# Three engines' orders rewritten in the second edge pipeline of a four-layer graph network

## What is computed

```python
x = layernorm(x + L0(x, edges, edge_attr_128))   # softmax-weighted messages, MLP
x = layernorm(x + L1(x, edges))                  # sum over edges, MLP, batch norm
x = layernorm(x + L2(x, edges, edge_attr_20))    # filtered messages, dense o1, shifted softplus, dense o2
x = layernorm(x + L3(x, edges))                  # two mean-aggregating convolutions
```

## Time and profile before

| | us |
|---|---|
| median of 3 runs (lowest to highest) | 2390.36 (2384.64 to 2391.72) |
| the profiled execution, its own time | 2387.5 |
| its span in the trace | 2385.8 |
| busy, TensorE / VectorE / ScalarE / GpSimd | 2083.7 / 1989.8 / 1791.3 / 1516.3 |

### The profile page before, as it was taken

The page is one execution under the profiler, slowest core; times in us unless marked ns, Lnnn a source line. Parts: engine busy times, 40 slices in busy tenths (PEclk is TensorE's granted clock), DMA queues, the critical chain, the costliest instruction groups (busy, mean ns, idle before and its releaser), DMA issues. The chain is left out here.

```text
span 2385.8 us, 45628 instructions
## 1 busy us (share of the span) xinstructions
PE 2083.7 (87%) x14016; PEld 1738.5 (73%) x14016; DVE 1989.8 (83%) x2942; ACT 1791.3 (75%) x3691; POOL 1516.3 (64%) x1114
## 2 busy tenths in 40 slices
PE   5999999999998899998998788888799998486664
PEld 4999999999997677775776677777566676365564
DVE  7999999999997666666997899999688888398564
ACT  4989999988997577775775788888699998375221
POOL 6888766777730544430777778870288884688787
PEclk9999999999999899997999899999899999699776
DMA  4777666655665888885886788885376765786653
GB/s 111 149 167 159 157 168 168 165 152 157 184 185 173 216 254 252 254 255 178 206 214 144 164 191 196 194 203 152 107 194 191 196 189 153 163 213 161 167 166 99
DMA packets 322548, 427.40 MB, mean 179 GB/s; under 512 B 113684, under 2 KB 169590, under 8 KB 322309
## 3 DMA queue, kind: packets, MB, share of 16 engines
q1 hardware_dynamic: 210004, 367.20, 54.9%
q0 software_dynamic: 112000, 56.93, 13.9%
q10 hardware_dynamic: 304, 0.36, 0.0%
HBM read 239.24 MB, written 185.90 MB: 178 GB/s over the span
## 5 line engine op out<-in xcount | busy, mean ns | idle before, releaser
L1784 POOL DMA_INDIRECT acc<-combined,first_ x100 | 212.4, 2124 | 87.8 <-issue 42.5
L510 PE MATMUL banks<-mats,g_hT 128*125 128x256 f32 x1000 | 258.6, 381 | 0.0
L529 PE MATMUL banks<-mats,g_zT 128*125 128x128 f32 x2000 | 238.8, 273 | 0.0
L529 PEld LDWEIGHTS banks<-mats,g_zT 128*125 128x125 f32 x2000 | 228.1, 188 | 0.0
L844 POOL DMA_INDIRECT gin_xs<-x,from_ x100 | 126.0, 1260 | 160.6 <-DMA x_of_src<-gin_xs 136.6
L1846 POOL DMA_INDIRECT em_y<-acc,from_ x100 | 141.2, 1412 | 128.2 <-PE banks L1949 98.3
L510 PEld LDWEIGHTS banks<-mats,g_hT 128*125 128x125 f32 x1000 | 189.3, 189 | 28.3 <-issue 0.2
L1012 DVE TENSOR_TENSOR gin_acc<-gin_acc,gin_qr 125x512 f32<-125x512 f32 x125 | 86.6, 693 | 117.1 <-ACT gin_qr L974 117.1
L590 ACT ACTIVATE g_zT<-banks,cols 128x500 f32<-128x500 f32 x250 | 179.1, 776 | 2.6 <-PE banks L518 2.6
L573 ACT ACTIVATE g_sq<-banks 125x512 f32<-125x512 f32 x250 | 144.9, 590 | 42.9 <-PE banks L510 42.5
L437 POOL DMA_INDIRECT g_xd<-in_x,idx x100 | 124.1, 1241 | 72.8 <-PE banks L544 46.0
(11 more groups left out here) (408 smaller groups left out, 6608.4 us busy)
## 6 DMA issues: line engine op xcount, KB each, us to landing
acc<-g_zero SPq DMA_DIRECT2D x126, 224.0 KB
x<-g_x SPq DMA_DIRECT2D x125, 224.0 KB
g_x<-in_xT SPq DMA_DIRECT2D x100, 250.0 KB
gin_x<-x SPq DMA_DIRECT2D x50, 448.0 KB
h<-gin_hr SPq DMA_DIRECT2D x50, 448.0 KB
al_h<-h SPq DMA_DIRECT2D x38, 448.0 KB
al_x<-x SPq DMA_DIRECT2D x38, 448.0 KB
out<-al_out SPq DMA_DIRECT2D x38, 448.0 KB
```

The lines of the kernel that those rows point to most:

```text
L510: m = nc.tensor.matmul(bank[0:P, 256 * j:256 * j + 256], HT[q % 2][:, c:c + P], K.W1c, start=False, stop=j == 1)
L529: m = nc.tensor.matmul(pO[q % 2][0:P, D * j:D * j + D], ZT[q % 2][:, h, P * j:P * j + P], K.W2[:, h, :], start=False, stop=j == R - 1 and ...
L1784: pool.indirect_dma_start(out=K.acc, out_offset=bass.IndirectOffsetOnAxis(ap=K.first[:, g, r:r + 1], axis=0), in_=CR[:, g, r * D:r * D + D ...
```

## The change

The three lists are permuted and some lags change; no piece is added, removed or edited.

```diff
@@ -2041,8 +2041,8 @@
                         m = nc.tensor.matmul(pC[0:P, D * j:D * j + D], HT[k % 2][:, P * j:P * j + P], K.W("W2rT"), start=False, stop=j == R - 1)
                     m.then_inc(cs, 1)
 
-                steps(EG, [(0, turn), (0, turn_y), (0, turn_back), (1, turn_x3), (0, first), (0, turn_yd), (1, hidden), (1, turn_x3d),
-                           (0, first_d), (1, back_h), (1, second), (0, update), (1, hidden_d), (0, update_d), (1, back_hd)])
+                steps(EG, [(1, update_d), (0, turn), (2, back_hd), (0, turn_y), (0, turn_back), (1, turn_x3), (0, first),
+                           (0, turn_yd), (1, hidden), (1, turn_x3d), (0, first_d), (1, back_h), (1, second), (0, update), (1, hidden_d)])
 
             @block.scalar
             def _(act):
@@ -2116,13 +2116,13 @@
                     nc.scalar.activation(flat(HR[k % 2]), pH[0:P, :], ACT.Copy).then_inc(hr, 1)
 
                 nc.scalar.preload_act_table_set("natural_log_exp_and_others")
-                steps(EG, [(0, relu_b), (1, lambda k: nbd.square(act, k, flat(BD[k % 3]), bd)), (2, lambda k: nc_.exp(act, k, done)), (0, copy_y),
-                           (1, nbd.log_of(act)), (1, lambda k: nbd.exp(act, k, x3d)), (1, copy_x3),
-                           (0, lambda k: na.square(act, k, flat(A[k % 2]), a)), (0, size), (0, copy_yd), (0, expo), (1, relu_h), (0, log),
-                           (0, size_d), (0, na.log_of(act)), (0, lambda k: na.exp(act, k, x2)), (1, copy_x3d), (0, expo_d), (0, log_d),
-                           (1, rows_h), (1, lambda k: nc_.square(act, k, pC[0:P, :], cs)),
-                           (0, lambda k: nb.square(act, k, flat(B[k % 3]), b)), (1, relu_hd), (0, nb.log_of(act)),
-                           (0, lambda k: nb.exp(act, k, x3)), (1, nc_.log_of(act))])
+                steps(EG, [(0, relu_b), (1, lambda k: nbd.square(act, k, flat(BD[k % 3]), bd)), (2, lambda k: nc_.exp(act, k, done)),
+                           (0, copy_y), (1, nbd.log_of(act)), (1, lambda k: nbd.exp(act, k, x3d)), (1, copy_x3),
+                           (0, lambda k: na.square(act, k, flat(A[k % 2]), a)), (0, size), (0, copy_yd), (1, relu_h), (0, expo),
+                           (0, na.log_of(act)), (0, log), (0, size_d), (0, lambda k: na.exp(act, k, x2)), (1, copy_x3d), (0, expo_d),
+                           (0, log_d), (1, lambda k: nc_.square(act, k, pC[0:P, :], cs)),
+                           (0, lambda k: nb.square(act, k, flat(B[k % 3]), b)), (1, rows_h), (1, relu_hd), (0, nb.log_of(act)),
+                           (1, nc_.log_of(act)), (0, lambda k: nb.exp(act, k, x3))])
 
             @block.vector
             def _(dve):
@@ -2203,9 +2203,9 @@
                     past(dve, hT, k)
                     nc.vector.tensor_tensor(C(k), banked(pC), nc_.times(k), ALU.mult).then_inc(done, 1)
 
-                steps(EG, [(1, apply_b), (1, nbd.reduce_of(dve)), (0, residual), (1, apply_bd), (1, sums), (0, positive), (1, average),
-                           (2, apply_c), (0, na.reduce_of(dve)), (0, soft), (0, positive_d), (0, apply_a), (0, join),
-                           (0, soft_d), (1, nc_.reduce_of(dve)), (0, nb.reduce_of(dve)), (0, join_d), (1, rows_hd)])
+                steps(EG, [(1, apply_b), (2, rows_hd), (1, nbd.reduce_of(dve)), (2, apply_c), (0, residual), (1, apply_bd),
+                           (0, na.reduce_of(dve)), (0, positive), (1, sums), (1, average), (0, soft), (0, apply_a), (0, positive_d),
+                           (0, join), (0, soft_d), (1, nc_.reduce_of(dve)), (0, nb.reduce_of(dve)), (0, join_d)])
 
 
 def edges_last(nc, K, out):
```

## The result

The changed kernel takes **2378.51 us** (median of 5 runs, 2376.88 to 2384.11), the kernel before 2390.36 beside it; ratio 0.9949, 95% interval 0.9932 to 0.9966. The prediction was 2396.4, so it was wrong in its sign: 0.5% faster, not 0.25% slower; that the time lies inside the range of 2376 to 2402 is owed to the rival that the range took in. The profiled execution has a span of 2376.7, its own time is 2378.4.

The account below looks back on a forecast made before the run. A 13.16 us step through TensorE, ScalarE and VectorE, with GpSimd ending the stage: pipeline some 12 us earlier, GpSimd 6 later, so 2387.5 becomes 2393.5, or 2396.4 from the median 2390.36; range 2376 to 2402.

Parts of the forecast that it names:

- the rival that the range took in: On GpSimd: it still makes 8 DMAs a step and the kernel takes 2376.7 us; chance 0.20.
- The ring: Second edge pipeline, `relu_b` to next `relu_b` through TensorE, ScalarE and VectorE: the step falls from 13.16 to 12.59 us.
- its two terms: In the step: `back_hd` leaves the chain, 0.44 us less; `positive` goes ahead of the scan, 0.13 us less.
- What was priced at nothing: ScalarE's list, `update_d`'s wait and later stores and loads cost nothing; bound 0 to 0.1 us a step.
- The first scatter: On GpSimd, the stage's first scatter comes 4.6 us earlier, at 1721.9 instead of 1726.52.
- The tail: GpSimd's scatters 20 to 24 each wait 3.78 us for the landing before, not for VectorE; stage ends at 2049.0.
- GpSimd's pace: VectorE's two-operand SBUF operations hold GpSimd's DMAs: 7 a step, not 8, at 1.80 us each instead of 1.64.
- The chain of accesses: GpSimd's DMAs after a scan, held by scan, `apply_a` and `apply_b`, return at 12.68 us, inside the next scan.
- GpSimd keeps up: If `apply_a` starts 0.25 us later, GpSimd makes 8 DMAs a step; end 13.7 us earlier, 2376.7; chance 0.20.
- One sign of two that were to make me wrong: On GpSimd: 8 DMAs in a step, or scatters at the end that wait for VectorE.

Follow-up runs that it names:

- e1: The kernel before with only TensorE's list new, the other two old: step 12.72 us, time 2384.74 us (1 run).
- e2: The kernel before with only VectorE's list new, the other two old: step 13.05 us, time 2383.53 us (1 run).
- e4: The kernel before with TensorE's and VectorE's lists new, ScalarE's old: step 12.62 us, time 2375.81 us, ratio to before 0.9934.
- e8: The changed kernel unaltered, run again for a second trace: 2380.29 us, ratio to the kernel before 0.9954.
- e5: The changed kernel with `positive_d` moved one place ahead of `apply_a` on VectorE: 2377.56 us, ratio to the kernel before 0.9941.
- e7: The changed kernel with `apply_c` moved one place back on VectorE, behind `residual`: 2394.56 us, ratio to the kernel before 1.0014.

## Why the prediction was wrong

- **The ring: right.** 12.59 forecast, 12.62 measured; its two terms, 0.44 and 0.13, are e1's 0.44 and e2's 0.11. VectorE's last `apply_c` ends 11.5 earlier (2033.12 to 2021.66; forecast 12).
- **What was priced at nothing: right.** No new wait stands in the ring; ScalarE's list is worth nothing (e4).
- **The first scatter: right.** 1721.9 forecast, 1722.15 measured.
- **The tail: right in kind.** Scatters 20 to 24 wait for landings, not for VectorE; 2.8 to 5.0 us each, 3.74 on average, where one row had given 3.78. The near match is in part luck: in e8 the five take 3.16 on average. From the end of scatter 19 to the stage's end it is 48.2 us, forecast 47.7.
- **GpSimd's pace: the step that failed.** "Either way 7 DMAs fit in a step, not 8, 1.80 us each" rests on a hold that begins with the operation. The chain of accesses came back to the scan at 12.68 of 12.59, that is 0.09 into it, and there it is free. The chain itself was right: it is there, hold for hold, from 1825.04 to 1837.43, but the free DMA at its end breaks the lock, and every chain of 7 is followed by one of 8. The pace is 1.666 (7.6 a step); 156 x 0.134 is 20.9 us, and the whole miss of the stage's end is 18.8 (2049.0 less 2030.2); the rest of the program, 3.7 us longer in this trace, brings the miss of the profiled execution down to 15.1 (2393.5 less 2378.4). The margin of 0.09 us between "held 1.1" and "not held" was the number to price, with both outcomes; the prediction gave the end of an operation as an edge and took its start for one without a row that showed it.
- **The rival "GpSimd keeps up": near in the time (2376.7 against 2378.5), not in its reason.** It wanted `apply_a` 0.25 later. `apply_a` starts 2.47 after the scan (2.46 worked out). And GpSimd does not keep up wholly: its scatters at the end do not wait for VectorE. One sign of two that were to make me wrong came, and that in 12 of 20 steps: 8 DMAs a step.

## What to carry to other kernels

When two engines run in lockstep with a period near each other's, the order of one sets a pace for the other that jumps by a whole instruction a step (7 or 8 here, or the two by turns) at margins of 0.1 to 0.2 us; price both sides of such an edge, and take no edge for known that no row lies near. Before believing that a list is worth its change, run the lists one by one: here two of three carried everything, and the third alone cost 0.86 us a step. And an operation that reads PSUM or a reduction, put between two that read both operands from SBUF, is a gap through which GpSimd's DMAs pass: e5 and e7 are each one moved operation away from the changed kernel, and 20 us of stage apart.

## What the runs showed of the hardware

An operation of VectorE with two operands in SBUF (0.65 to 1.26 us) held every indirect DMA on GpSimd that started 0.05 to 0.45 us after the operation's recorded start (563 of 563), and none that started between 0.10 before and 0.02 after that start (0 of 146); between the two some were held (13 of 32). Where it held none, VectorE's operation was sometimes the one that lengthened, by 0.08 at most. Operations with one operand in PSUM, and reductions, held none: of the 1282 DMAs in the fourteen traces with such an operation running 0.11 us after their start, none took over 1.23 us. The landing of four scatters, between the end of the last issue and the start of the next scatter, took 2.7 to 5.0 us in these tails.
